# Relative scores and transposes of an attention kernel, moved to column strips of 32

## What is computed

```
x = x + attention(layernorm(x));  x = x + ffn(layernorm(x))

idx   = clip(pos[None, :] - pos[:, None], -20, 20) + 20
attn1 = einsum('bhqd,bhkd->bhqk', q, k)
attn2 = einsum('bhqd,qkd->bhqk', q, rel_k[idx])
attn  = softmax((attn1 + attn2) / sqrt(8), axis=-1)
w1    = einsum('bhqk,bhkd->bhqd', attn, v)
w2    = einsum('bhqk,qkd->bhqd', attn, rel_v[idx])
out   = (w1 + w2) heads joined @ Wo.T + bo
```

## Time and profile before

| what | us |
|---|---|
| median of three runs | 1352.57 |
| lowest and highest run | 1350.77, 1354.61 |
| span of the profiled execution | 1351.2 |
| TensorE busy with matmuls | 1265.6 |
| TensorE busy with loads of weights | 937.2 |
| VectorE busy | 915.5 |
| ScalarE busy | 758.2 |
| GpSimd busy | 571.5 |

### The profile page before, as it was taken

The page is one execution under the profiler, slowest core; times in us unless marked ns, Lnnn a source line. Parts: engine busy times, 40 slices in busy tenths (PEclk is TensorE's granted clock), DMA queues, the critical chain, the costliest instruction groups (busy, mean ns, idle before and its releaser), DMA issues. The chain is left out here.

```text
span 1351.2 us, 67633 instructions
## 1 busy us (share of the span) xinstructions
PE 1265.6 (94%) x30688; PEld 937.2 (69%) x30688; DVE 915.5 (68%) x1780; ACT 758.2 (56%) x1414; POOL 571.5 (42%) x1047
## 2 busy tenths in 40 slices
PE   4888599999999999999999999999999999999998
PEld 3555267777777777777777777777777777766766
DVE  5766776767767767676767767676777776346664
ACT  5767155656656656565656656566666565633232
POOL 5876345343434443443435353434344444212221
PEclk9988589999999999999999999999999999999999
DMA  4656310111011111102020111121111110013231
GB/s 133 196 189 200 82 30 19 47 31 56 25 49 40 36 45 29 50 27 53 22 56 26 56 37 46 38 57 29 54 36 39 44 32 9 13 50 87 78 87 47
DMA packets 101542, 76.99 MB, mean 57 GB/s; under 512 B 13256, under 2 KB 97032, under 8 KB 101256
## 3 DMA queue, kind: packets, MB, share of 16 engines
q1 hardware_dynamic: 101256, 72.67, 18.2%
HBM read 44.86 MB, written 26.21 MB: 53 GB/s over the span
## 5 line engine op out<-in xcount | busy, mean ns | idle before, releaser
L1107 DVE TENSOR_REDUCE b_mx<-b_a 128x1 f32<-128x512 f32 x1024 | 658.6, 685 | 233.0 <-PE b_a L828 227.4
L1052 ACT ACTIVATE b_p<-b_s 128x512 f32<-128x512 f32 x1024 | 570.0, 596 | 402.4 <-PE b_s L869 316.1
L919 PE MATMUL b_pv<-b_p,vg 128*16 128x128 f32 x8192 | 286.8, 275 | 0.0
L788 POOL TENSOR_TENSOR qd<-q,one 48x512 bf16<-48x512 bf16 x256 | 266.7, 1042 | 27.7 <-POOL b_np L770 5.1
L869 PE MATMUL b_s<-qd,z 112*128 112x32 bf16 (+1 forms) x6016 | 249.1, 189 | 2.2 <-issue 2.0
L765 POOL TENSOR_TENSOR b_np<-b_db,one 128x16 bf16<-128x16 bf16 x192 | 39.3, 266 | 470.5 <-DVE b_mx L1107 467.3
L828 PE MATMUL b_a<-k,q 48*128 48x512 bf16 x1024 | 202.8, 393 | 27.1 <-DVE b_mx L1107 11.6
L869 PEld LDWEIGHTS b_s<-qd,z 112*128 112x128 bf16 x6016 | 205.9, 99 | 12.6 <-issue 2.6
L919 PEld LDWEIGHTS b_pv<-b_p,vg 128*16 128x16 f32 x8192 | 196.3, 96 | 21.1 <-issue 0.2
L854 PE MATMUL b_s<-q,k 54*128 54x64 bf16 (+3 forms) x4608 | 188.0, 201 | 4.5 <-issue 1.3
L854 PEld LDWEIGHTS b_s<-q,k 54*128 54x128 bf16 (+1 forms) x4608 | 126.5, 95 | 90.1 <-PE b_s L854 29.0
(11 more groups left out here) (142 smaller groups left out, 1241.7 us busy)
## 6 DMA issues: line engine op xcount, KB each, us to landing
x<-in_x SPq DMA_DIRECT2D x32, 256.0 KB, 3.3
scratch_qop<-a_parts SPq DMA_DIRECT2D x16, 384.0 KB, 2.5
scratch_kop<-a_parts SPq DMA_DIRECT2D x16, 384.0 KB, 3.1
k<-scratch_kop SPq DMA_DIRECT2D x32, 192.0 KB
q<-scratch_qop SPq DMA_DIRECT2D x32, 192.0 KB
scratch_v<-a_vr SPq DMA_DIRECT2D x16, 256.0 KB, 3.2
k<-scratch_kop SPq DMA_DIRECT2D x32, 128.0 KB
q<-scratch_qop SPq DMA_DIRECT2D x32, 128.0 KB
```

The costliest lines, as they stand in the source:

```text
L788: nc.gpsimd.tensor_tensor(dst, src, one, ALU.mult).then_inc(s["qd_ready"], 1)
L919: nc.tensor.matmul(PV[32 * a:32 * a + V16, g * P:(g + 1) * P], v[:, 0 if t <= i else 1, t, h, :], PR[at.c % 2][:, t, h, :], start=(t == 0 ...
L1052: nc.scalar.activation(out, src, ACT.Exp, scale=SCALE).then_inc(s["p_ready"], 1)
L1107: nc.vector.tensor_reduce(MX[v.c % 2][:, h:h + 1], PA[(n + hp) % NBANK][:, :], AX_X, ALU.max, negate=True).then_inc(s["a_used"], 1)
```

## The change

It moves four things of stage_attend onto other parts of the array.

- **Relative scores** use column strips. A matmul of relative_block has 32 columns of z as weights and writes 32 keys. Beside the diagonal the ten blocks of a sub-chunk all lie in one strip (the last of the tile before, the first of the tile behind). On the diagonal a bank holds one query strip s = 2g + n of 32 queries; diagonal_jobs lists for each key strip the blocks that are near enough to it, and the lists are issued in turns over the strips. For s = 0 and 3 these are 16 + 10 blocks, for s = 1 and 2 16 + 16 + 10: 26 + 42 = 68 in each sub-chunk. The table z gets 64 more columns.
- **Scores on the diagonal** go through head_scores and both_halves as the others do: 16 matmuls of 32 columns on row halves, L828's pair, the wait for `half`, and 16 more with the banks swapped. TensorE waits once, ahead of them, for the second of its banks; before, it waited bank by bank. `s_ready` still comes bank by bank.
- **The guard transpose** is three matmuls with the bf16 identity, on strips, into f32.
- **The output transposes** are 16 plain f32 matmuls on strips; their moving operand is 36 columns of the identity (nine of each 32: eight channels and the row sum). normalise reads them from there.

The places named in the diff as @@ are of the whole kernel; cut to its core:

```
@@ -49,6 +49,9 @@
+STRIP = 32
+NSTRIP = P // STRIP
+HDS = HD + 1
@@ -57,7 +60,7 @@
-ZLO_W = ZLO_0
+ZLO_W = ZLO_0 + P // 2
@@ -645,19 +648,28 @@
-    def beside(t, i):
-        return abs(t - i) == 1
-
-    def blocks(t, i, g):
-
-        half = P // QB // 2
-        near = {0: range(half * g, half * (g + 1)), -1: range(REL // QB), 1: range((P - REL) // QB, P // QB)}
-        return near.get(t - i, range(0))
+    def beside_blocks(t, i):
+
+        return {-1: range(REL // QB), 1: range((P - REL) // QB, P // QB)}[t - i]
+
+    def query_strip(g, n):
+
+        return 2 * g + n
+
+    def diagonal_jobs(s, strip):
+
+        jobs = []
+        for b in range(s * STRIP // QB, (s + 1) * STRIP // QB):
+            above = STRIP * strip - (QB * b + QB - 1) < REL
+            below = STRIP * (strip + 1) - 1 - QB * b > -REL
+            if above if s < NSTRIP // 2 else below:
+                jobs.append((b, strip))
+        return jobs
...
@@ -836,13 +848,16 @@
                 t, g, i, p = c // NG, c % NG, at.c % T, (at.c // T) % 2
-                rows = DROW if t <= i else ROWS
+                out = SC[bank_of(at, 2 * c + n)]
+                rows, hhs = DROW if t <= i else ROWS, range(HH // NG * g, HH // NG * (g + 1))
+                if t == i:
+                    s = query_strip(g, n)
+                    rows, hhs, w, q0, col = (ROWS if s < NSTRIP // 2 else DROW), range(HH), STRIP, STRIP * s, lambda hh: (2 * hh + hp) * STRIP
+                elif window(t, i):
+                    w, q0, col = 64, 64 * n, lambda hh: (2 * hh + hp - HG * g) * 64
...
@@ -854,45 +869,37 @@
-            def relative_scores(at, c, bank=None):
+            def relative_block(at, c, n, b, strip, heads, nq, x0):
+
+                r = slice(STRIP * strip, STRIP * (strip + 1))
+                o = SC[bank_of(at, 2 * c + n)][r, :].rearrange("p (h q) -> p h q", q=nq)[:, :, QB * b % nq:QB * b % nq + QB]
+                return nc.tensor.matmul(o, k["z"][0:QROWS, x0 - QB * b + STRIP * strip:x0 - QB * b + STRIP * (strip + 1)],
+                                        QD[at.c % 2][0:QROWS, heads[0]:heads[-1] + 1, b * QB:(b + 1) * QB],
+                                        start=False, stop=True, skip_group_check=True)
+
+            def relative_scores(at, c):
...
-                    ins = nc.tensor.matmul(o, k["z"][0:QROWS, x0:x0 + P],
-                                           QD[at.c % 2][0:QROWS, heads[0]:heads[-1] + 1, b * QB:(b + 1) * QB],
-                                           start=False, stop=True, skip_group_check=True)
-                return ins
-
-            def diagonal_scores(at, c, n):
-
-                g, i, p = c % NG, at.c % T, (at.c // T) % 2
-                q0, r = i * P + 64 * g + 32 * n, slice(0, HALF + ROWS)
-                for hh in range(HH):
-                    nc.tensor.matmul(SC[bank_of(at, 2 * c + n)][:, hh * 64:(hh + 1) * 64], K[p][r, hh, i * P:(i + 1) * P],
-                                     Q[p][r, hh, :, q0:q0 + 32], start=hh == 0, stop=True, skip_group_check=True)
+                if t != i:
+                    x0 = (ZLO_0 if t < i else ZLO_W + ZHI_0) + (t - i) * P
+                    for b in beside_blocks(t, i):
+                        ins = relative_block(at, c, QB * b // 64, b, NSTRIP - 1 if t < i else 0, range(HG * g, HG * g + HG), 64, x0)
+                    ins.then_inc(s["s_ready"], 2)
+                    return
+                for n in range(2):
+                    lists = [diagonal_jobs(query_strip(g, n), strip) for strip in range(NSTRIP)]
+                    x0 = ZLO_W + ZHI_0 if query_strip(g, n) < NSTRIP // 2 else ZLO_0
+                    for b, strip in [one[m] for m in range(max(map(len, lists))) for one in lists if m < len(one)]:
+                        ins = relative_block(at, c, n, b, strip, range(H), STRIP, x0)
+                    ins.then_inc(s["s_ready"], 1)
 
             def scores(at, c):
...
-                if t == i:
-                    for n in range(2):
-                        if at.since(1) or 2 * c + n >= NBANK:
-                            pe.wait_ge(s["p_ready"], freed(at, 2 * c + n))
-                        if n == 0:
-                            row_pairs_ahead(at, c)
-                        diagonal_scores(at, c, n)
-                        relative_scores(at, c, n).then_inc(s["s_ready"], 1)
-                    return
                 if at.since(1) or c >= 1:
                     pe.wait_ge(s["p_ready"], freed(at, 2 * c + 1))
...
                 both_halves(at, c, (1, 0), False)
-                relative_scores(at, c).then_inc(s["s_ready"], 2)
+                relative_scores(at, c)
@@ -947,12 +954,19 @@
                 pe.wait_ge(s["mp_ready"], at.count(1, 1))
-                nc.tensor.transpose(MIB, NP[:, :, :, :].rearrange("p hp c hh -> p (hp c hh)"), idb[:, :]).then_inc(s["mt_ready"], 1)
+                parts = NP[:, :, :, :].rearrange("p hp c hh -> p (hp c hh)")
+                for strip in range(6 * H // STRIP):
+                    r = slice(STRIP * strip, STRIP * (strip + 1))
+                    ins = nc.tensor.matmul(MI[r, 0:P], parts[:, r], idb[:, :], start=True, stop=True)
+                ins.then_inc(s["mt_ready"], 1)
 
             def output_transposes(at):
                 pe.wait_ge(s["xt_ready"], at.count(1, 1))
+                keep = k["ident"][:, :].rearrange("p (a c) -> p a c", a=NQ4)[:, :, 0:HDS]
                 for g in range(NQ4):
-                    ins = nc.tensor.transpose(MI[:, g * P:(g + 1) * P], XT[:, g * P:(g + 1) * P], k["ident"][:, :])
+                    for strip in range(NSTRIP):
+                        ins = nc.tensor.matmul(MI[STRIP * strip:STRIP * (strip + 1), g * NQ4 * HDS:(g + 1) * NQ4 * HDS],
+                                               XT[:, g * P + STRIP * strip:g * P + STRIP * (strip + 1)], keep, start=True, stop=True)
                 ins.then_inc(s["xtt_ready"], 1)
```

More of the change, by code:

```diff
@@ L646, in window @@
         return abs(t - i) <= 1
-    def beside(t, i):
-        return abs(t - i) == 1
-    def blocks(t, i, g):
-        half = P // QB // 2
-        near = {0: range(half * g, half * (g + 1)), -1: range(REL // QB), 1: range((P - REL) // QB, P // QB)}
-        return near.get(t - i, range(0))
+    def beside_blocks(t, i):
[10 more added lines that the diff above has]
+        return jobs
     def halves_done(at, c):
-        done = [sum(beside(t, i) for t in range(T)) * NG for i in range(T)]
-        here = sum(beside(n // NG, at.c % T) for n in range(c + 1))
+        done = [sum(window(t, i) for t in range(T)) * NG for i in range(T)]
+        here = sum(window(n // NG, at.c % T) for n in range(c + 1))
         return at.it * (PER // T * sum(done)) + (at.c // T * sum(done) + sum(done[:at.c % T]) + here)
@@ L838, in head_scores @@
                 t, g, i, p = c // NG, c % NG, at.c % T, (at.c // T) % 2
-                rows = DROW if t <= i else ROWS
-                r = slice(HALF * hp, HALF * hp + rows)
[L841 to L845, removed]
+                out = SC[bank_of(at, 2 * c + n)]
[5 more added lines that the diff above has]
+                    w, q0, col = 64, 64 * n, lambda hh: (2 * hh + hp - HG * g) * 64
+                else:
+                    w, q0, col = P, 0, lambda hh: (hh - HH // NG * g) * P
+                r = slice(HALF * hp, HALF * hp + rows)
                 return [(out[:, col(hh):col(hh) + w], K[p][r, hh, t * P:(t + 1) * P],
@@ L978, in first_row_transposes @@
                 ins.then_inc(o["xT"], 1)
-            MIB = MI[0:6 * H, 0:P // 2].bitcast(BF16)
             for n, (u, hh) in enumerate(order[:HH + EARLY]):
@@ L1043, in exponentials @@
                         src = src.rearrange("p (h q) -> p h q", h=H)
-                        q0 = 64 * g + 32 * n
-                        out = PR[at.c % 2][:, t, :, q0:q0 + 32]
+                        q0 = STRIP * query_strip(g, n)
+                        out = PR[at.c % 2][:, t, :, q0:q0 + STRIP]
                     elif window(t, i):
@@ L1057, in guard_copy @@
                     act.wait_ge(s["m_in"], at.count(32))
-                nc.scalar.copy(MT[:, :], MI[0:6 * H, 0:P // 2].bitcast(BF16)).then_inc(s["mt_copied"], 1)
+                nc.scalar.copy(MT[:, :], MI[0:6 * H, 0:P]).then_inc(s["mt_copied"], 1)
             def output_copy(at):
@@ L1119, in normalise @@
                 dve.wait_ge(s["xtt_ready"], at.count(1, 1))
-                v = MI[:, :].rearrange("p (n c) -> p n c", c=32)
-                nc.vector.reciprocal(RD[:, :], v[:, :, HD]).then_inc(s["rd"], 1)
+                out = MI[:, 0:H * HDS]
+                nc.vector.reciprocal(RD[:, :], out.rearrange("p (n c) -> p n c", c=HDS)[:, :, HD]).then_inc(s["rd"], 1)
                 dve.wait_ge(s["rd"], at.count(1, 1))
@@ L1125, in normalise @@
                 xn = XN[at.c % 2][:, :].rearrange("p (a g d) -> p g a d", a=NQ4, d=HD)
-                nc.vector.tensor_tensor(xn, MI[:, :].rearrange("p (g a c) -> p g a c", g=NQ4, a=NQ4)[:, :, :, 0:HD],
```

(1 more changed line is left out.)

## The result

| | median us | lowest to highest |
|---|---|---|
| before (4 runs) | 1351.67 | 1348.38 to 1354.61 |
| after (4 runs) | 1498.40 | 1494.38 to 1504.21 |

The ratio is 1.1096, 95% interval 1.1069 to 1.1124: the change costs 11%. The forecast was 1500 us.

A forecast was written before the change was run, and what follows sets the result against it. TensorE's order sets the time before, instruction supply after: 4.64 blocks at 3.88 us plus 0.2 make 18.2 us a unit against 15.88, +2.32 times 64 = +148 us, giving 1500 us; range 1400 to 1550, 77 to 80%.

The forecast's parts named there:

- The mechanism and the count: TensorE's instructions arrive in blocks of about 127 matmuls, one block ahead; 39264 matmuls, about 310 packets, stops put down to "issue".
- The array's cost: Diagonal sub-chunk, if instructions came at once: 1.78 us instead of 1.88, twice a unit, -0.20 us.
- The output transposes: End of a unit: 0.41 us instead of 0.59, half counted because of a wait for an exponential, -0.09 us a unit.
- The price of a block: TensorE's instruction supply: 3.88 us per block of 127 matmuls, 4.64 blocks making 18.0 us a unit.
- The sub-chunks off the diagonal: Slower than block supply at 37 ns a record, only part of the difference caught up: +0.2 us a unit.
- The new waits for a score bank: Diagonal sub-chunks now ask for their second bank before starting: 0.05 us a unit.
- The first rival: Blocks come faster than the four stops say and TensorE's work alone sets the time: 1326 us; chance 11%.
- The fifth rival: Stops over a microsecond let TensorE's clock fall, or blocks take over 4.05 us: above 1550 us; chance 4%.

The follow-up runs named there:

- burst over four strips: Kernel before with bursts added after its last matmul; this one, 1280 matmuls of 16 columns in turns over four strips, took 33.4 us.
- d_narrow: Changed kernel with the diagonal's 136 relative scores for 4 of 16 heads, 8 columns each instead of 32: 1558.85 us, ratio 1.1499.
- x_beside: Kernel before with only the relative scores beside the diagonal on one key strip, no matmul added: 1346.09 us, ratio 0.9942.
- d_wide: Changed kernel with each relative score of the diagonal streaming 128 columns instead of 32, same matmul count: 1510.39 us, ratio 1.1165.

## Why the prediction was right

- **The mechanism and the count** were right: 39264 matmuls, 308 packets (310 expected), stops of "issue" one block apart, VectorE and ScalarE with more idle time. ScalarE's exponentials now wait longer for TensorE's scores:

```profile
L1065 ACT ACTIVATE b_p<-b_s 128x512 f32<-128x512 f32 x1024 | 564.8, 596 | 539.3 <-PE b_s L876 468.3
```

- **The array's cost** was right where it could be seen: 1.69 us for a diagonal sub-chunk with g = 0; with g = 1 (604.73 to the first L941 at 606.62) 1.89; 1.79 between them, where 1.78 was forecast. Over the 40 sub-chunks that no stop interrupts the medians are 1.69 and 1.88. Eight pairs of half-row scores took 0.22 (0.23). The strips overlap: 67 relative scores in 0.96 us.
- **The output transposes** were mis-sized: 612.40 to 613.18 is 0.78 us, 0.47 of it the transposes, where 0.41 was forecast, and 0.31 a wait for an exponential, as the earlier trace rows had warned. Alone, the part costs 6 us instead of bringing 64 x 0.09.
- **The price of a block was too high.** 3.88 us was the mean of the four full blocks that the trace of before showed; the 108 of after give 3.70, and a core with no other traffic 3.47 to 3.75. The four stood where queries are loaded, with a DMA share of 0.20 to 0.24. The blocks of after, sorted by that share, last 3.62 us below 0.05, 3.69 up to 0.20 and 3.80 above, each lot spread from 3.4 to 3.9 or 4.3: so traffic may account for about half of the 0.18, and the rest stays open. The prediction's argument that traffic had not stretched them looked at the packet alone, which is under a third of the price. 4.64 x 0.18 x 64 = 53 us too many.
- **The sub-chunks off the diagonal were undercounted.** A unit is 18.06 us and 4.64 x 3.70 = 17.2, so 0.9 us a unit is not block price, where 0.2 was put down: 45 us too few. The stops show where it is. In the stage, 107 blocks between two stops took 3.70 us each; the other 183, in stretches of two to six without a stop, took 738 us, 4.03 each, and 183 x 0.33 / 64 = 0.9 us. One stretch of after, mostly off the diagonal, between two stops:

```profile
611.17:621.32 10.15, 8.73 (x254) 1.00 0.29 72
```

  Two blocks last 10.15 us here, 2.7 more than their price. TensorE is at its own pace, and since a block is asked for only when the one before it begins, what is slow here isn't made up in the next diagonal: each block costs its own work or the price, whichever is more, while the prediction compared them as means over a unit.

- **The new waits for a score bank** were put at 0.05 us a unit. Waits for an exponential are 8.6 + 5.0 = 13.6 us in 800, 0.31 a unit, against 2.7 or 0.05 before. They are part of the 0.9, as far as no block was awaited at the same time.

The two large errors cancel to 8 us. That the forecast of 1500 came within 2 us of 1498.4 is luck: the mechanism was known to some per cent, not to 0.1%.

The first rival (1326 us) fell. It was also what the Trainium skill implies (Runtime: NRT & Kernel Launch, section Instruction fetch mechanics): fetching is hidden because dispatch is slower than the fill. The burst over four strips contradicts it for short matmuls on strips, with 2.5 us of standstill in every 3.75; the page's block of 256 instructions agrees with the 128 matmuls and loads between two stops. The fifth rival, a falling clock, hardly occurred in after (0.99 in the stage), but d_narrow showed how near it is.

## What to carry over

Count TensorE's instructions as well as its columns. Here a matmul with its weights costs about 29 ns of supply (3.70 us / 127; 27 where stops stand 3.47 us apart), whatever it streams, once the block in store is used up; splitting one into several small ones pays only while the stretch stays above that, and it is the dense stretch of a block or two that counts, not the mean. A narrower weight tile that leaves the number of matmuls alone and saves a change of tiling (x_beside) is free; and more useful columns in a matmul whose supply is the limit are free as well (d_wide: some 118 us of work for 9).

## What the runs showed that was not expected

- In the burst over four strips, 128 matmuls of 16 columns ran in 1.2 us at 1.2 GHz, some 8 ns apart; on one strip 3.56 us, 27 ns apart. The Trainium skill (TensorE: Matmul & The Clock Gate, section Wait — 56ns, not 53.3ns?) puts the least distance of two starts at about 25 ns: the one strip agrees, and the figure does not hold for matmuls that go in turns over different strips.
- The distance between two stops comes in steps: 3.47, 3.75, 4.02 us, some 0.27 apart, with and without traffic. What makes the steps stays open.
- Less work per matmul cost 55 us through the clock (d_narrow).
